# A node one-hot stored tile by tile: strided writes on VectorE, contiguous weights on TensorE

## What is computed

```python
q = (h @ Wq + bq).reshape(N, DH, NH)              # 3125 nodes, 8 heads of 64
k = (h @ Wk + bk).reshape(N, DH, NH); v = k
scores = jnp.einsum('edh,edh->eh', q[rows], k[cols])   # one score per edge and head
ex = jnp.exp(scores - m[rows]); attn = ex / denom[rows]
out = jax.ops.segment_sum(attn[:, None, :] * v[cols], rows, num_segments=N)
```

## Time and profile before

| | us |
|---|---|
| median of three runs | 2060.45 |
| lowest and highest run | 2049.58, 2065.38 |
| span of the profiled execution (first to last instruction) | 2055.2 |
| attention stage in it, first to last `node_hot` | 278.2 to 1185.5 |
| busy in the span: PE, DVE, ACT, POOL | 1634.7, 1427.3, 1155.5, 1110.8 |

### The profile page before, as it was taken

How to read it: one execution, slowest core, us unless ns; L and a number is a source line. 1 busy time by engine, 2 the same in 40 slices (tenths; PEclk the granted TensorE clock), 3 DMA queues, 4 the chain that set the end, 5 groups by cost and what they waited for, 6 DMA issues and landing times.

```text
span 2055.2 us, 23478 instructions
## 1 busy us (share of the span) xinstructions
PE 1634.7 (80%) x5301; PEld 1039.7 (51%) x5301; DVE 1427.3 (69%) x2551; ACT 1155.5 (56%) x3820; POOL 1110.8 (54%) x1346
## 2 busy tenths in 40 slices
PE   5999837887787887778778887863888888788888
PEld 2444426666666666666666664431444444334444
DVE  7999848778777777777877773671556666546664
ACT  3554356887887877868878782330333433233333
POOL 0000057677676776776767722346466666646661
PEclk9999969889989889888988889976898899899999
DMA  8222275545545545555455418546466767756762
GB/s 191 90 91 90 90 217 147 162 151 159 173 132 158 170 139 157 157 155 159 144 164 171 143 49 204 151 135 192 135 200 200 200 201 201 202 158 195 200 200 87
DMA packets 133316, 324.76 MB, mean 158 GB/s; under 512 B 42024, under 2 KB 42274, under 8 KB 133160
## 3 DMA queue, kind: packets, MB, share of 16 engines
q0 software_dynamic: 70240, 229.93, 38.2%
q1 hardware_dynamic: 62920, 93.17, 16.8%
HBM read 283.86 MB, written 39.16 MB: 157 GB/s over the span
## 4 chain that ended last, share of the span: by engine, by line
PE 29%; DVE 26%; issue 21%; another core or an unknown queue 13%; ACT 4%; DMA 4%; DVEq 1%; POOL 1%; SPq 0%; ACTq 0%; POOLq 0%
PE wide L855 12%; PE sums L911 6%; DVE nodes L1411 5%; PE wide L940 5%; DVE nodes L1402 3%; DVE late_rows L1527 2%; ACT heads L776 2%; DMA h2tab<-node 2%; PE sums L1012 2%; DVE ohT L1310 2%; ACT wide L781 1%; DVE nodes L1359 1%; PE wide L850 1%; PE wide L868 1%
## 5 line engine op out<-in xcount | busy, mean ns | idle before, releaser
L697 ACT ACTIVATE nodes<-arena,nodes 128x64 f32<-128x64 f32 x2840 | 684.3, 332 | 7.2 <-issue 4.7
L541 POOL DMA_INDIRECT arena<-ktab,idx x425 | 413.5, 973 | 270.7 <-DVEq L1406 146.6
L911 PE MATMUL sums<-nodes,oh 128*125 128x260 f32 x1768 | 495.4, 425 | 69.2 <-DVE nodes L1359 69.2
L541 POOL DMA_INDIRECT late_rows<-h2tab,idx x425 | 403.6, 950 | 244.8 <-issue 138.0
L855 PE MATMUL wide<-w_sb,node 128*125 128x512 f32 x1000 | 490.9, 635 | 28.8 <-ACT node L767 14.4
L911 PEld LDWEIGHTS sums<-nodes,oh 128*125 128x125 f32 x1768 | 360.2, 209 | 143.0 <-DVE nodes L1359 77.6
L940 PE MATMUL wide<-q_win,ohT 125*128 125x512 f32 x850 | 315.3, 502 | 57.7 <-DVEq L1410 54.9
L1402 DVE TENSOR_TENSOR nodes<-wide,arena 128x1024 f32<-128x1024 f32 (+1 forms) x225 | 258.8, 1160 | 113.5 <-PE wide L940 50.2
L855 PEld LDWEIGHTS wide<-w_sb,node 128*125 128x125 f32 x1000 | 195.2, 202 | 257.8 <-issue 236.0
L940 PEld LDWEIGHTS wide<-q_win,ohT 125*128 125x128 f32 x850 | 225.3, 308 | 94.1 <-DVEq L1410 65.3
L1411 DVE TENSOR_REDUCE nodes<-nodes 128x16 f32<-128x1024 f32 (+1 forms) x225 | 256.9, 1151 | 0.0
(11 more groups left out here) (187 smaller groups left out, 1608.5 us busy)
## 6 DMA issues: line engine op xcount, KB each, us to landing
near_lists<-node_tab SPq DMA_DIRECT2D x27, 531.2 KB
q_win<-qtab SPq DMA_DIRECT2D x26, 448.0 KB
qtab<-q_win SPq DMA_DIRECT2D x17, 448.0 KB
arena<-ktab,idx POOLq DMA_INDIRECT x425
late_rows<-h2tab,idx POOLq DMA_INDIRECT x425
h2tab<-node POOLq DMA_DIRECT2D x25, 250.0 KB, 2.9
node<-h2tab SPq DMA_DIRECT2D x26, 224.0 KB
attn_tab<-kept_sums SPq DMA_DIRECT2D x25, 227.5 KB
```

What stands on the lines that cost most here:

```text
L541: gp.indirect_dma_start(into[:, b, t, :], None, tab, bass.IndirectOffsetOnAxis(ap=idx[:, b, t:t + 1], axis=0)).then_inc(s["rows_in"][b][PA ...
L697: last = act.activation(msgs[:, t, h // HH, h % HH * DH:(h % HH + 1) * DH], rows[:, 1 - b, t, h * DH:(h + 1) * DH], ACT.Copy, scale=den_in ...
L911: last = pe.matmul(halves[:, u, :], oh[:, 1 - b, t, :], rhs[side][:, t, u, :], start=t == 0, stop=t == CT - 1)
```

## The change

`ohT` is kept tile by tile: column `t * 128 + p` holds edge `p * 17 + t`. VectorE still reads `near` straight through and makes the same 2176 elements a partition in one instruction, but its consecutive writes now lie 128 elements (512 bytes) apart, in 128 runs of 17. TensorE's weights for tile `t` are 128 neighbouring elements. The number of instructions, the waits, all DMAs and all other tiles stay.

```diff
                         for part in range(SPLIT):
-                            last = pe.matmul(wide[n % 2][:, (t - t0) * D:(t - t0 + 1) * D], ohT[:, :].rearrange("p (e t) -> p t e", t=CT)[:, t, :],
+                            last = pe.matmul(wide[n % 2][:, (t - t0) * D:(t - t0 + 1) * D], ohT[:, t * 128:(t + 1) * 128],
                                              q_win[:, b, part, :], start=part == 0, stop=part == SPLIT - 1)
@@
             def node_hot(g, b):
 
-                dve.tensor_scalar(ohT[:, :], near[:, b, :], node_id[:, b:b + 1], None, ALU.is_equal).then_inc(ohT_ready, 1)
+                dve.tensor_scalar(ohT[:, :].rearrange("n (t p) -> n p t", t=CT), near[:, b, :].rearrange("n (p t) -> n p t", t=CT), node_id[:, b:b + 1], None, ALU.is_equal).then_inc(ohT_ready, 1)
```

## The result

Over 20 executions of each kernel, the changed one takes 2070.72 us (median, 2048.72 to 2100.38) against 2057.02 us for the kernel before (2035.83 to 2083.61). The ratio is 1.0066, with a 95% interval of 1.0037 to 1.0096: slower by 13.7 us at the medians, and within the 1% that counts as no change. 2071.5 was forecast. The number fits better than its parts do: one term was too small by 11 us, another, taken as nothing, gave back about as much, and the stage that was changed grew by less than the time did.

The account below looks back on a forecast made before the run. The prediction took VectorE's in-order stream, with node_hot on it, to set each attention turn. Longer node_hot +20.4, merge waits -5.1 and weight loads -4.2 made +11.1 us on 2060.45, so 2071.5 us; range 2048 to 2122.

Parts of the forecast that it names:

- The bound: Attention loop: VectorE runs each turn in program order and never rests before node_hot, so time added there lengthens the turn.
- The write's price: node_hot's store with the large step: 0.95 ns an element, 2.20 us, 0.85 us more; +20.4 us over 24 chunks.
- The idea of two streams: node_hot on VectorE: two streams side by side would halve the large step's price of 1.90 ns an element.
- The rule of the Trainium skill: VectorE's node_hot: full rate needs runs of two adjacent words; estimated 3.9 to 5.6 us, or 2.0 to 2.9 at half.
- What the merge gives back: VectorE's waits at L1372 for the former chunk's sums, 9.7 us in all, absorb node_hot's growth in six chunks: -5.1 us.
- The waits before group 6: VectorE waiting for TensorE's queries before group 6: 18 waits, 38 us in all, expected to stay near 38.
- rival 3: TensorE's groups 5 and 6 return to 2.4 GHz, up to 38 us of waits come back, 2033.5 us; chance 0.14.
- The weights: TensorE's L940 loads: 0.117 us shorter each, mostly hidden; only groups 5 and 6 in 18 chunks gain, -4.2 us.
- Group 4: VectorE's group 4 product starts some 11.1 us after group 0; its wait moves along and hides nothing added before.
- The sum: Whole kernel: +20.4 - 5.1 - 4.2 = +11.1 us on 2060.45, giving 2071.5 us.

Follow-up runs that it names:

- e3_twice: Kernel before with the node_hot compare made twice in a row, a wait between; 2070.18 us, ratio 1.0109.
- e12: Changed kernel with node_hot cut into the edges of 127 partitions and those of the last; 1903.42 us, 82 us over the kernel before on that chip.
- the repetition: The changed kernel run once more, unedited, beside the kernel before; 2063.34 us, ratio 1.0026.
- e2: Kernel before's write of ohT with the change's contiguous weight reads (edges mixed, same work); 2049.46 us, ratio 0.9983.
- e6: Kernel before with node_hot made by ScalarE in two steps instead of VectorE's compare; 2047.17 us, ratio 1.0003.
- e5: Kernel before with POOL issuing three gathers ahead of its one-hot work instead of seven; 2071.92 us, ratio 1.0159.
- e11_before_again: The kernel before, unedited, on a third chip; 1821.39 us.

## Why the prediction was right

**The bound.** VectorE's stream sets the turn, and its `node_hot` lies on it with nothing ahead to wait for: right. e3_twice shows it, since time at that place alone makes the loss. Not all that is added there arrives: in the loop of after 6.8 of 31.1 us did.

**The write's price.** The step that was mis-sized: 0.95 ns an element was taken, 1.156 is measured ((2651 - 136) / 2176). +1.30 us a chunk instead of +0.85, 24 x 0.45 = 10.8 us too little. The idea of two streams fits the read (0.955), and the store in part (1.75 to 1.156). The rule of the Trainium skill that was weighed (Vector Engine (DVE) Microarchitecture Reference, section 5.2, Measured stream behaviour on trn2) named the danger rightly: single words far apart cost here too. The estimate from its figures was 3.9 to 5.6 us, and 2.0 to 2.9 at half of them; the measured 2651 ns lie in the halved one, and e12 with 3911 ns for 2159 elements at the low end of the other.

**What the merge gives back.** -5.1 us forecast, -8.3 measured (9.7 to 1.4). The mechanism was right, and with the larger price it gave more.

**The waits before group 6.** The step that failed: they were kept near 38 us "unchanged", and fell to 20.6, in the repetition to 26.2. That is 17.4 us, or 11.8, given back, a good part of what rival 3 described. In the chunk shown, groups 5 and 6 ran at a granted clock of 1.00 instead of 0.53. e2 (36.6 with contiguous weights) says that the weights alone don't do it, e3 (28.6 without) that added time does some of it. That both together do more is possible (20.6 to 27.6 in four profiles, 32.9 and 28.6 over strided weights) and not shown. Nor is it simply that a longer `node_hot` helps: e6, with none on VectorE, has 13.9. Why fewer chunks then run at the low clock is not settled.

**The weights.** -4.2 us forecast; e2 measured -3.5, with nothing in its interval as well. That loads hide is shown (235 and 232 ns apart). That the gain comes out of the waits before group 6, as the forecast had it, is not: in e2 these fell by 1.4 us.

**Group 4.** It was to start some 11.1 us after group 0 whatever comes before it: 11.14 us in the chunk of after, and 11.13 as the median of the 25 chunks in both kernels. Right, and so it swallowed nothing of `node_hot`'s growth: 48.9 us before, 50.6 after.

**The sum.** +11.1 forecast; +13.7 at the medians and +11.5 in the repetition (by the ratios +13.6 and +5.3). The loop, which is what the sum counts, grew by 6.8 and 1.6 us in the two profiles. The two errors, +10.8 of work missing and some 12 to 17 of returned waits missing, nearly cancel. With the right price alone the forecast would have been 20.4 + 10.8 - 8 - 4.2 = +19; with the returned waits as well it would have been +2 to +7, which is what the loop did. In the profile the rest of the difference came from the untouched stage (+11.0); where the medians have theirs from, one profile of each can't say. So the sign was right for the stated reason, VectorE's longer instruction, and that the time lies within 1 us of the forecast is luck.

**What stays open.** What the wait before group 4 is: TensorE's last recorded matmul for it ends 2.77 us before the product starts (719.34 + 1.29 = 720.63 to 723.40), the profile calls it "remote", POOL's order moves it, and one chip doesn't have it. One thing the traces show about it: it ends when a burst of transfers does. In the chunk of before the DMA engines are at 0.89 while it lasts, and at 0.05 right behind it:

```profile
712.70:716.63 3.93, 2.05 (x10) 1.52 (x8) 1.93 (x2) 3.93 (x18) 3.56 (x5) 1.00 0.89 297
```

So it is in 22 of the 23 waits of over 0.5 us before group 4 in that profile: in the stretch from 0.5 to 2 us behind their end the DMA share is under 0.3. In e5, where the wait stands before the merge, it is so in 22 of 24. A full DMA alone doesn't make the wait, though: on the third chip there is none in the chunk that has this stretch,

```profile
632.00:637.00 5.00, 5.00 (x26) 4.39 (x24) 5.00 (x6) 5.00 (x22) 4.36 (x7) 1.00 1.03 314
```

and no run separates the two, so this is a coincidence in time and not a shown cause. Also open is why the untouched stage varies.

## What to carry to other kernels

Time at the head of an in-order stream that sets the turn is paid, less what the waits behind it give back, and here these gave back from a third to all of it. A weight load behind matmuls of 512 columns was hidden: leave the long step to TensorE's weights. If VectorE must take it, try an even outermost count, and a read with the step rather than a write (0.955 against 1.156 ns an element here). Judge such a change by its own stage, as work added against waits given back: the rest of the kernel can vary by more than the change brings.

## What the runs showed of the hardware

- A compare from 16-bit to 32-bit words costs, beside some 136 ns that are fixed, 0.56 ns an element with both sides contiguous, 0.955 with a read step of 34 bytes and 16 rows, 1.83 with 17 rows; 1.156 with a store step of 512 bytes and 128 rows, 1.75 with 127 (and an odd run of 2159 on the read side).
- A weight load of 128 columns takes 302 ns with a step of 17 words and 189 ns contiguous, and that changes the distance of neighbouring matmuls of 512 columns by 3 ns (235 to 232).
- Chips differ: the same kernel takes 1821.39 us on one and 2051.85 and 2056.35 us on two others. The DMAs of the second layer moved 232 GB/s there and 188 here, and VectorE's waits in the loop were 12.5 us there and 119.2 here, with the same instruction times. The granted clock in the second layer was 1.00 there and 0.88 here. The window of the second layer in e11_before_again, to be held against the one of before above:

```profile
1280.00:1800.00 520.00, 490.29 (x1456) 248.45 (x1457) 358.63 (x500) 223.56 (x315) 388.83 (x411) 1.00 0.80 232
```
